# Gated products woven into the second attention of a two-layer gated cross-attention kernel

## The chip, the cores and the metric

The kernel runs on one core of a Trainium2 chip. The metric is the device time of one execution in microseconds (us). Three runs of the kernel before took 686.56, 687.71 and 687.75 us; the median, 687.71, is what a changed kernel is held against.

## What is computed

Two layers work on x (2 batches of 1024 tokens, 256 features) with a context of 77 tokens. All numbers are fp32. Cut to what matters:

```python
x = x + tanh(g_xattn[0]) * differential_attention(ctx, layernorm(x))       # layer 0: 32 half heads of 8
x = x + tanh(g_ffn[0]) * zone_ffn(layernorm(x))                            # router takes 3 of 8 zones, gelu, 1024 wide
x = x + tanh(g_xattn[1]) * (softmax(q @ k.T / 4) @ v @ Wo + bo)            # layer 1: 16 heads of 16, q from layernorm(x)
x = x + tanh(g_ffn[1]) * ((silu(gate) * up) @ wd.T)                        # gate = x @ wg.T, up = x @ wu.T, 768 wide,
                                                                           # int weights times 1/127, x normed
```

## The kernel before

**Tiles and stages.** The 2048 tokens are four tiles of 512 (J = 4); a tile is four blocks of 128 tokens. The stages are ATT0, FFN0, ATT1 and FFN1. A product in fp32 precision is made of three passes over parts rounded to fp32r: high times high, low times high, high times low (`product`, L1163, its matmuls at L1167). So each operand has a high part, written by ScalarE (ACT) as a copy, and a low part, raw minus high, written by VectorE (DVE).

**What sets the order.** `plan()` (L118) writes one list of steps by hand. Each engine walks through the whole list and issues its share of every step in that order, with semaphores between the engines. A step moved in the list is moved on every queue. `attention_tile` (L74) lays out one tile of an attention: eight `attend` units of two heads, and after each second unit a `values` and an `outputs` step of the pair before; `side` holds steps that come after a given unit and `fillers` steps that are spread over the gaps. `weave` (L59) does the same for the zone and gated stages.

**The second attention, steps by engine.** `attend` is two matmuls of 512 columns into one of two pairs of score banks, SC (L1302); ACT takes their exp into a probability buffer PB of 77 rows (L815). `values` is 32 matmuls of 128 columns on 32-column tiles into PV bank 0 (L1187); DVE transposes it (`outputs`, L1059) and takes reciprocals (`mix`, L1065); GpSimd (POOL) adds the output bias to x ahead of the first mix of a tile (L686) and multiplies (L692). `max` is two matmuls of 154 columns (L1274) and a DVE reduction (L1051); `negmax` turns the maxima (L1285), ACT copies them and SP moves them into the query tile. `query` makes twelve matmuls, and `q_move` moves its parts on the DMA queues of SP (L543), for tile 2 of this attention half of them on POOL (L659). `turn_mix` is eight transposes of the attention result, `project` 24 matmuls of 256 columns with Wo and an addition on DVE (L1127). For the norm ahead of FFN1, `stats` and `norm` are on DVE and POOL (L969, L982, L630), `scale` is four activations (L760), `turn` eight transposes, two copies and two low parts.

**The gated stage.** Its weights come as int32 by `ffn_load` (L582), into one of two buffers, and are split in six halves by `ffn_split` (ACT L884, DVE L911). A `gated` step s works on one of six chunks of a tile: twelve matmuls for gate and up into a pair of SC banks, silu on ACT (L892), a product on DVE (L1142), its high part on ACT (L728) and its low part on DVE (L911), and two steps later the down product, six matmuls into PV (`gated_out`, L1204). `evac` copies the sums with the gate's factor (L874), `out` turns them back with eight transposes (L1352), adds to x (L1114), and SP stores the tile (L587).

**Banks.** PSUM has eight banks: SC four, PV two, AUX two. Turns, queries, maxima and the like go through a ring of auxiliary banks: AUX 0, AUX 1 and PV 1 in the attentions, the two AUX in the zone and gated stages.

**What the change touches.** In `plan()` the whole second attention and gated stage, L213 to L257; the ring of banks, L275 to L289; in the engines' programs the branches `ffn_load`, `out`, `mix`, `attend`, `ffn_split`, `gated`, `turn`, `query`, `turn_mix`, `project` and the helpers `bank`, `fill`, `attend_values`, `gated_out`, `gated_hi`. The order before, from plan(), of the first steps behind the third attend of tile 2 was: max, norm, attend, max, values, max, outputs, max, ffn_split, scale, attend; no gated step came before the last values of tile 3.

## Time and profile before

| | us |
|---|---|
| median of three runs | 687.71 |
| the profiled execution, its own time | 686.08 |
| its span, first to last instruction | 684.2 |
| second attention: first attend to first gated matmul | 484.4 to 568.6 |
| gated stage, to its last matmul | 568.6 to 678.4 |
| evac, out and store of the last tile | 678.4 to 684.2 |

The profiled execution is one more run; its span is its time less what lies around the instructions. In the rows, PE is the matrix engine (PEld its weight loads, which overlap it), ACT ScalarE, DVE VectorE, POOL GpSimd, SP the engine that only issues DMAs. PEclk is the granted clock of PE as a share of 2.4 GHz. "idle before <-" is how long an engine stood idle ahead of an instruction and who released it; L numbers are lines of the kernel before.

### The profile page before, as it was taken

How to read it: one execution, taken by the hardware profiler on the slowest of the kernel's cores; microseconds unless marked ns; L12 is line 12 of the kernel's file. 1: busy time of each engine (PE TensorE's matmuls, PEld its weight loads, DVE VectorE, ACT ScalarE, POOL GpSimd, SP SyncE). 2: the span in 40 equal slices, each digit the busy share in tenths (PEclk: the TensorE clock that was granted, in tenths of full speed). 3: DMA queues.
4: the chain of work that ended last, by engine and by line, in shares of the span. 5: the costliest groups of instructions: out<-in, count | busy, mean ns of one | idle time of the engine just before them, and what ended most of it. 6: DMA issues, size and time to landing. Idle time of an engine off the chain costs nothing.

```text
span 684.2 us, 10256 instructions
## 1 busy us (share of the span) xinstructions
PE 621.6 (91%) x3676; PEld 479.4 (70%) x3676; DVE 369.2 (54%) x817; ACT 370.0 (54%) x631; POOL 142.6 (21%) x212
## 2 busy tenths in 40 slices
PE   2699888898799999999999999999789889999996
PEld 2575555554478888888887787778577767888885
DVE  6677667779573524335456435443477655343332
ACT  4316757566775746556657445446746564243232
POOL 9633265354640000000000000001245222000000
PEclk9769999999999999999999999999978699999999
DMA  7320120112130030300312430000343000000000
GB/s 229 97 77 21 32 60 11 46 49 97 31 122 4 0 124 0 123 2 0 124 32 62 94 123 2 2 0 2 94 140 94 3 2 1 1 31 1 32 31 32
DMA packets 21970, 34.68 MB, mean 51 GB/s; under 512 B 4640, under 2 KB 13216, under 8 KB 21920
## 3 DMA queue, kind: packets, MB, share of 16 engines
q1 hardware_dynamic: 19648, 30.51, 14.3%
q0 software_dynamic: 1984, 3.44, 2.2%
q8 instruction: 30, 0.49, 0.3%
q14 instruction: 20, 0.16, 0.1%
q10 hardware_dynamic: 288, 0.07, 0.0%
HBM read 18.93 MB, written 2.10 MB: 31 GB/s over the span
## 4 chain that ended last, share of the span: by engine, by line
PE 76%; DVE 8%; POOL 6%; ACT 6%; issue 3%; DMA 0%; DVEq 0%; ACTq 0%; POOLq 0%
PE SC L1167 28%; PE PV L1167 26%; PE PV L1187 5%; PE AUX L1167 4%; PE SC L1302 4%; PE AUX L1274 3%; ACT XN L760 2%; DVE NM L1051 2%; DVE O L1059 2%; PE AUX L1230 2%; PE PV L1274 1%; POOL RSTD L630 1%; DVE ST L969 1%; ACT PB L815 1%; POOL QG L659 1%
## 5 line engine op out<-in xcount | busy, mean ns | idle before, releaser
L911 DVE TENSOR_TENSOR HL<-HF,HH 128x512 fp32r<-128x512 f32 x120 | 83.7, 698 | 154.1 <-ACT HH L857 153.8
L815 ACT ACTIVATE PB<-SC 77x1024 f32<-77x1024 f32 x96 | 94.3, 1014 | 46.5 <-PE SC L1302 46.2
L857 ACT ACTIVATE HH<-PV 128x512 fp32r<-128x512 f32 x96 | 57.3, 597 | 66.8 <-PE SC L1167 66.8
L852 ACT ACTIVATE HF<-PV 128x512 f32<-128x512 f32 x96 | 57.3, 597 | 54.8 <-PE PV L1167 53.0
L630 POOL TENSOR_TENSOR RSTD<-RSTD,NHALF 128x4 f32<-128x4 f32 x16 | 17.4, 1089 | 321.8 <-DVE RSTD L982 321.7
L1167 PE MATMUL PV<-XH,WAH 128*128 128x512 f32 x192 | 77.7, 404 | 1.0 <-DVE O L1059 1.0
L1167 PE MATMUL SC<-HH,WBH 128*128 128x512 f32 x192 | 76.3, 397 | 0.0
L1167 PE MATMUL SC<-HH,WBL 128*128 128x512 f32 x192 | 75.7, 394 | 0.0
L1167 PE MATMUL PV<-XL,WAH 128*128 128x512 f32 x192 | 75.4, 393 | 0.0
L1167 PE MATMUL PV<-XH,WAL 128*128 128x512 f32 x192 | 75.3, 392 | 0.0
L1167 PE MATMUL SC<-HL,WBH 128*128 128x512 f32 x192 | 74.9, 390 | 0.0
L1302 PE MATMUL SC<-QG,KA 128*128 128x512 f32 x192 | 67.9, 444 | 4.2 <-ACT PB L815 3.1
L1051 DVE TENSOR_REDUCE NM<-AUX 128x4 f32<-128x308 f32 x139 | 62.0, 465 | 11.3 <-PE AUX L1274 11.3
L1274 PE MATMUL AUX<-KA,QG 96*128 96x154 f32 (+1 forms) x192 | 51.0, 335 | 10.2 <-DVE NM L1051 6.0
L1274 PEld LDWEIGHTS AUX<-KA,QG 96*128 96x128 f32 x192 | 37.1, 211 | 27.8 <-DVE NM L1051 12.2
L1187 PE MATMUL PV<-PB,V 128*32 128x256 f32 (+1 forms) x1024 | 54.5, 345 | 1.7 <-DVE O L1059 1.6
L892 ACT ACTIVATE SG<-SC 128x512 f32<-128x512 f32 x24 | 14.3, 596 | 68.7 <-PE SC L1167 68.7
L1142 DVE SCALAR_TENSOR_TENSOR HF<-SC,SG 128x512 f32<-128x512 f32 x24 | 16.6, 692 | 59.8 <-ACT SG L892 59.8
L1302 PEld LDWEIGHTS SC<-QG,KA 128*128 128x128 f32 x192 | 33.0, 204 | 13.9 <-issue 7.7
L1187 PEld LDWEIGHTS PV<-PB,V 128*32 128x32 f32 (+1 forms) x1024 | 28.0, 114 | 21.0 <-issue 9.6
L1167 PEld LDWEIGHTS PV<-XH,WAH 128*128 128x128 f32 x192 | 36.1, 188 | 8.6 <-issue 1.8
L1167 PEld LDWEIGHTS SC<-HH,WBL 128*128 128x128 f32 x192 | 36.0, 188 | 8.7
(241 smaller groups left out, 1214.8 us busy)
## 6 DMA issues: line engine op xcount, KB each, us to landing
QG<-QH SPq DMA_DIRECT2D x96, 64.0 KB, 2.0
WSA<-in_wa SPq DMA_DIRECT2D x6, 1024.0 KB, 5.1
...
```

Of the source, the lines that this page charges most:

```text
L630: pool.tensor_tensor(RSTD[:, 1, :], RSTD[:, 0, :], NHALF[:, :], ALU.pow).then_inc(pool_step, 1)
L815: act.activation(probs(n)[0:S, :, :], SC[0:S, n % 2, :, :], ACT.Exp, scale=SCALE[a]).then_inc(exp_done, 1)
L852: act.activation(HF[s % 2][:, :], PV[:, s % 2, :], ACT.Gelu_apprx_tanh)
L857: act.activation(HH[s % 2][:, :], PV[:, s % 2, :], ACT.Gelu_apprx_tanh).then_inc(act_done, 1)
L892: act.activation(SG[s % 2][:, :], SC[:, s % 2, 0, :], ACT.Silu, scale=DEQ).then_inc(silu_done, 1)
L911: return dve.tensor_tensor(dst, raw, hi.bitcast(F32), ALU.subtract)
L1051: dve.tensor_reduce(NM[:, n % 2, t, 4 * u:4 * u + 4], bank(key)[:, 0:4 * S].rearrange("p (h n) -> p h n", h=4), AX_X, ALU.max, negate=True ...
L1142: dve.scalar_tensor_tensor(HF[s % 2][:, :], SC[:, s % 2, 1, :], DEQ, SG[s % 2][:, :], ALU.mult, ALU.mult).then_inc(hf_ready, 1)
L1167: ins = pe.matmul(ps, lhs, rhs, start=start and i == 0, stop=stop and i == len(passes) - 1)
L1187: ins = pe.matmul(PV[32 * r:32 * r + 32, 0, at_h:at_h + P * (heads.stop - heads.start)], v, p[:, heads, :, r, :], start=True, stop=True)
L1274: ins = pe.matmul(ps[:, i * n_cols:(i + 1) * n_cols], QG[n % 2][0:ROWS, g, P * t:P * (t + 1)], KA[a][0:ROWS, j // 2, NS[a] * g:NS[a] * (g ...
L1302: ins = pe.matmul(SC[:, n % 2, i, :], KALL[a][:, at_h:at_h + P], QG[m % 2][:, h // NS[a], :], start=True, stop=True)
```

## The change

The steps `turn`, `query`, `turn_mix`, `project` and `out` are cut into their halves. The `gated` step becomes three: `gated_g` (six matmuls), `gated_u` (six matmuls) and `gated_mul`, and the down product a step `gated_out`. Behind attend 2 of tile 2 the list blends the gated steps 0 to 5 with the rest of tile 2 of the attention, then steps 6 to 11 with tile 3 and the attention's end, by the loads in LOAD; steps 12 to 23 follow alone. While they are woven, the attention has one pair of score banks (SC 0) and the gated steps the other (SC 1); the down sums go to PV 1 and AUX 1; the auxiliary ring is AUX 0 alone from the first down product to step 12, then AUX 0 and PV 0. Silu is computed from a tanh: SG = tanh(gate/2), then (SG + 1) * gate on DVE, then times up on DVE. The first two weight loads go into the last zone of FFN0, four of the six splits into tile 0, two into tile 1. The norm ahead of FFN1 comes two to three units after its project, and project, turn_mix come earlier. The values read all 128 rows, so POOL clears the rows from 64 on of the buffers at the end of FFN0. POOL's bias add waits for the norm of its tile and no longer for the reciprocals. The result is stored in eight halves instead of four tiles.

```diff
@@ -51,6 +51,9 @@
 ATT0, FFN0, ATT1, FFN1 = range(4)
 SMALL = 13
 LAG = 2
+MIXED = 2 * HC
+PARTS = {"turn": (3, KC), "query": (3, KC), "turn_mix": (2, KC), "project": (2, 2), "out": (3, 2)}
+LOAD = {"attend": 2, "values": 3, "max": 1, "negmax": 2, "turn": 2, "turn_mix": 2, "project": 3, "out": 2}
...
+def blend(main, items):
+
+    items, out, given = parted(items), [], 0
+    total = sum(LOAD.get(step[0], 0) for step in items)
+    for n, atom in enumerate(main):
+        out += atom
+        while items and (given * len(main) < total * (n + 1) or not LOAD.get(items[0][0], 0)):
+            given += LOAD.get(items[0][0], 0)
+            out.append(items.pop(0))
+    return out + items
+
+
+def gated_atoms(first, last):
+
+    atoms = []
+    for s in range(first, last):
+        atoms += [[("gated_g", s)], [("gated_u", s), ("gated_mul", s)]]
+        if s >= LAG:
+            atoms.append([("gated_out", s - LAG)])
+            if (s - LAG) % HC == HC - 1:
+                atoms[-1] += [("evac", FFN1, (s - LAG) // HC)]
+    return atoms
...
+    side.setdefault(per * (Z - 2) + FC + FC - 1 + LAG + 3, []).extend([("ffn_load", 0), ("ffn_load", 1)])
...
+    def at(side, u, *more):
+        side.setdefault(u, []).extend(more)
+    def behind(side, j, base):
+        at(side, base, ("turn_mix", j, 0))
+        at(side, base + 1, ("turn_mix", j, 1))
+        at(side, base + 2, ("project", j))
+        for i, step in enumerate(norm(FFN1, j)):
+            at(side, base + 3 + i // 3, step)
+        at(side, base + 5, ("scale", FFN1, j))
+    side = {}
+    at(side, 0, *norm(ATT1, 3))
+    at(side, 1, ("ffn_split", 0, 0))
+    at(side, 2, ("scale", ATT1, 3))
+    at(side, 3, ("q_move", 1, 2, 0), ("ffn_split", 0, 1), ("ffn_load", 2))
+    at(side, 4, ("turn", ATT1, 3))
+    at(side, 5, ("ffn_split", 1, 0))
+    at(side, 7, ("q_move", 1, 2, 1), ("ffn_split", 1, 1))
+    steps += attention_tile(1, 0, side, [], left)
+    side = {}
+    at(side, 1, ("ffn_split", 2, 0))
+    behind(side, 0, 1)
+    at(side, 3, ("ffn_split", 2, 1))
+    at(side, 4, ("negmax", 1, 2, 0))
+    at(side, 5, ("query", 1, 3))
+    at(side, 6, ("q_move", 1, 3, 0))
+    at(side, 7, ("negmax", 1, 2, 1))
+    steps += attention_tile(1, 1, side, [(maxima(1, 2, 0), 0, 3), (maxima(1, 2, 1), 4, 7)], left)
+    side = {}
+    at(side, 0, ("q_move", 1, 3, 1), ("turn", FFN1, 0, 0))
+    at(side, 1, ("turn", FFN1, 0, 1))
+    behind(side, 1, 1)
+    at(side, 5, ("negmax", 1, 3, 0))
+    at(side, 7, ("turn", FFN1, 1))
+    items = attention_tile(1, 2, side, [(maxima(1, 3, 0), 1, 5), (maxima(1, 3, 1), 5, 8)], left)
+    alone = items.index(("attend", 1, 2, 2)) + 1
+    steps += items[:alone] + blend(gated_atoms(0, HC), items[alone:])
+    side = {}
+    at(side, 0, ("negmax", 1, 3, 1))
+    behind(side, 2, 1)
+    at(side, 5, ("out", FFN1, 0, 0))
+    at(side, 6, ("out", FFN1, 0, 1))
+    at(side, 7, ("turn", FFN1, 2))
+    items = attention_tile(1, 3, side, [], left) + attention_end(left)
+    steps += blend(gated_atoms(HC, MIXED), items)
+    side = {}
+    at(side, 1, ("turn_mix", 3, 0))
+    at(side, 3, ("turn_mix", 3, 1))
+    at(side, 5, ("project", 3))
+    at(side, 6, *norm(FFN1, 3))
+    at(side, 7, ("out", FFN1, 1, 0))
+    at(side, 8, ("scale", FFN1, 3), ("out", FFN1, 1, 1))
+    at(side, 12, ("turn", FFN1, 3, 0))
+    at(side, 13, ("turn", FFN1, 3, 1))
+    at(side, 25, ("out", FFN1, 2, 0))
+    at(side, 26, ("out", FFN1, 2, 1))
+    for n, atom in enumerate(gated_atoms(MIXED, HC * J)):
+        steps += atom + side.get(n, [])
+    end = HC * J
+    steps += [("gated_g", end), ("gated_u", end), ("gated_mul", end), ("gated_out", end - 2), ("gated_out", end - 1),
+              ("evac", FFN1, 3), ("out", FFN1, 3)]
+    return parted(steps)
...
+    home, uses, turn_now, ring = {}, [0, 0, 0, 0], 0, (0, 1, 2)
+    lent, last_in = [], {}
     for step in PLAN:
         order[step] = seen.get(step[0], 0)
         seen[step[0]] = order[step] + 1
-        if step[0] in ("zone", "gated"):
-            banks = 2
+        if step[0] == "zone":
+            ring = (0, 1)
         elif step == ("attend", 1, 0, 0):
-            banks = 3
+            ring = (0, 1, 2)
+        elif step == ("gated_out", 0):
+            ring = (0,)
+        elif step == ("gated_g", MIXED):
+            ring = (0, 3)
...
-            return AUX[:, n, :] if n < 2 else PV[:, 1, :]
+            return AUX[:, n, :] if n < 2 else PV[:, 3 - n, :]
...
+        MIXED_UNITS = unit(1, 2, 0)
+        SUMS = (PV[:, 1, :], AUX[:, 1, :])
+
+        def scores(n):
+
+            return SC[:, n % 2 if n < MIXED_UNITS else 0, :, :]
+
+        def gate(s):
+
+            return SC[:, 1 if s < MIXED else s % 2, :, :]
...
                 elif kind == "ffn_load":
                     i = step[1]
-                    sp.wait_ge(y_done, ZSTEPS)
                     sp.wait_ge(zsplit_done, FC * Z)
                     if i == 2:
                         sp.wait_ge(fsplit_done, 2)
                     dst = WI[i % 2][:, :].rearrange("p (c n) -> p c n", c=HC if i == 2 else KC)
                     sp.dma_start(dst, chunks((wg, wu, wd)[i])).then_inc(ffn_in[i], 16)
                 elif kind == "out" and step[1] == FFN1:
-                    j = step[2]
-                    for i in range(2):
-                        used(sp, step + (i,))
-                    sp.dma_start(out[j], X[:, TT * j:TT * (j + 1), :]).then_inc(stored, 16)
-            sp.wait_ge(stored, 16 * J)
+                    _, _, j, i = step
+                    used(sp, step)
+                    sp.dma_start(out[j][:, 2 * i:2 * i + 2, :],
+                                 X[:, TT * j + 2 * i:TT * j + 2 * i + 2, :]).then_inc(stored, 16)
+            sp.wait_ge(stored, 16 * 2 * J)
...
+                elif kind == "zone_end":
+                    pool.wait_ge(rstd_ready, sum(NORMS.index(s) < NORMS.index(("norm", ATT1, 3)) for s in NORMS))
+                    pool.wait_ge(hl_ready, ZSTEPS)
+                    pool.memset(PB2[1][1][64:P, :, :], 0.0).then_inc(pb_set, 1)
+                    pool.memset(PB2[1][0][64:P, :, :], 0.0).then_inc(pb_set, 1)
+                    for s in range(2):
+                        pool.wait_ge(y_done, ZSTEPS - 1 + s)
+                        pool.memset(PB[0][64:P, s, :], 0.0).then_inc(pb_set, 1)
+                        pool.memset(PB[1][64:P, s, :], 0.0).then_inc(pb_set, 1)
+                    pool.wait_ge(pb_set, 10)
...
+                            pool.wait_ge(xn_ready, order["norm", ATT1, j] + 1)
...
+                        pool.wait_ge(rz_ready, n + 1)
...
-                        act.wait_ge(y_done, ZSTEPS)
-                    act.activation(probs(n)[0:S, :, :], SC[0:S, n % 2, :, :], ACT.Exp, scale=SCALE[a]).then_inc(exp_done, 1)
+                        act.wait_ge(pb_set, (9, 10, 10, 10)[n - A0_UNITS])
+                    act.activation(probs(n)[0:S, :, :], scores(n)[0:S, :, :], ACT.Exp, scale=SCALE[a]).then_inc(exp_done, 1)
...
                 elif kind == "ffn_split":
                     _, i, h = step
                     act.wait_ge(ffn_in[i], 16)
+                    act.wait_ge(y_done, ZSTEPS)
                     dst, src, rows = ffn_half(i, h)
                     act.activation(dst[0][:, rows, :], src, copy).then_inc(fsplit_hi, 1)
-                elif kind == "gated":
+                elif kind == "gated_u":
                     s = step[1]
-                    act.wait_ge(g_ready, s + 1)
-                    if s >= 2:
-                        act.wait_ge(hf_ready, s - 1)
-                    else:
-                        act.wait_ge(sc_ready, ALL_UNITS)
-                    act.activation(SG[s % 2][:, :], SC[:, s % 2, 0, :], ACT.Silu, scale=DEQ).then_inc(silu_done, 1)
                     if s:
-                        gated_hi(s - 1)
-                elif kind == "gated_end":
-                    gated_hi(GSTEPS - 1)
+                        act.wait_ge(hf_ready, s)
+                        if s >= 3:
+                            act.wait_ge(gy_done, s - 2)
+                        else:
+                            act.wait_ge(fsplit_done, 6)
+                        act.activation(GH[(s - 1) % 2][:, :], GF[(s - 1) % 2][:, :], copy).then_inc(ghh_ready, 1)
+                    if s < GSTEPS:
+                        act.wait_ge(g_ready, s + 1)
+                        if s >= 2:
+                            act.wait_ge(hf_ready, s - 1)
+                        else:
+                            filled(act, ("query", 1, J - 1, KC - 1))
+                        act.activation(SG[s % 2][:, :], gate(s)[:, 0, :], ACT.Tanh, scale=0.5 * DEQ).then_inc(tanh_done, 1)
...
+                elif kind == "gated_g":
+                    s = step[1] - 1
+                    if s >= 0:
+                        dve.wait_ge(ga_done, s + 1)
+                        dve.wait_ge(u_ready, s + 1)
                         if s >= 2:
                             dve.wait_ge(ghl_ready, s - 1)
                         else:
-                            dve.wait_ge(pv_done, ALL_UNITS // 2)
-                        dve.scalar_tensor_tensor(HF[s % 2][:, :], SC[:, s % 2, 1, :], DEQ, SG[s % 2][:, :],
+                            dve.wait_ge(fsplit_done, 6)
+                        dve.scalar_tensor_tensor(GF[s % 2][:, :], SG[s % 2][:, :], 0.5 * DEQ * DEQ, gate(s)[:, 1, :],
                                                  ALU.mult, ALU.mult).then_inc(hf_ready, 1)
+                elif kind == "gated_mul":
+                    s = step[1]
                     if s:
                         dve.wait_ge(ghh_ready, s)
                         if s >= 3:
                             dve.wait_ge(gy_done, s - 2)
-                        lo_part(HL[(s - 1) % 2][:, :], HF[(s - 1) % 2][:, :], HH[(s - 1) % 2][:, :]).then_inc(ghl_ready, 1)
+                        lo_part(GL[(s - 1) % 2][:, :], GF[(s - 1) % 2][:, :], GH[(s - 1) % 2][:, :]).then_inc(ghl_ready, 1)
+                    if s < GSTEPS:
+                        dve.wait_ge(tanh_done, s + 1)
+                        dve.scalar_tensor_tensor(SG[s % 2][:, :], SG[s % 2][:, :], 1.0, gate(s)[:, 0, :],
+                                                 ALU.add, ALU.mult).then_inc(ga_done, 1)
...
-                rows = slice(0, P) if a == 0 else slice(0, S)
                 for i in range(2):
-                    p = probs(2 * q + i)[rows, :, :].rearrange("s i (t q r) -> s i t q r", t=TT, r=32)
+                    p = probs(2 * q + i)[:, :, :].rearrange("s i (t q r) -> s i t q r", t=TT, r=32)
                     for n in range(1 if a == 0 else 2):
                         heads = slice(0, 2) if a == 0 else slice(n, n + 1)
                         at_v = (j // 2 * (D // DV) + (2 * k + i if a == 0 else 4 * k + 2 * i + n)) * (DV + 1)
-                        v = VALL[a][rows, at_v:at_v + 32]
+                        v = VALL[a][:, at_v:at_v + 32]
...
-                        pe.wait_ge(pv_out, ALL_UNITS // 2)
-                        used(pe, LENT[1][-1])
+                        for n in (1, 2):
+                            used(pe, last_in[n])
...
-                    ins = product(PV[:, c, :], [(WNH[:, f, cols], WNL[:, f, cols], HH[s % 2][:, :], HL[s % 2][:, :])],
+                    ins = product(SUMS[c], [(WNH[:, f, cols], WNL[:, f, cols], GH[s % 2][:, :], GL[s % 2][:, :])],
...
+                    if n > MIXED_UNITS:
+                        pe.wait_ge(exp_done, n)
...
+                elif kind in ("gated_g", "gated_u") and step[1] < GSTEPS:
+                    cols = slice(P * f, P * (f + 1))
+                    if kind == "gated_g":
+                        if f == 0:
+                            pe.wait_ge(fsplit_done, 4)
+                            for c in range(KC):
+                                used(pe, ("turn", FFN1, j, c))
+                        if s in (0, MIXED):
+                            pe.wait_ge(exp_done, ALL_UNITS if s else MIXED_UNITS)
+                        else:
+                            pe.wait_ge(ga_done, s if s < MIXED else s - 1)
+                        product(gate(s)[:, 0, :], [(WGH[:, c, cols], WGL[:, c, cols], XH[:, j, c, :], XL[:, j, c, :])
+                                                   for c in range(KC)]).then_inc(g_ready, 1)
+                        if s not in (0, MIXED):
+                            pe.wait_ge(hf_ready, s if s < MIXED else s - 1)
+                        product(gate(s)[:, 1, :], [(WUH[:, c, cols], WUL[:, c, cols], XH[:, j, c, :], XL[:, j, c, :])
+                                                   for c in range(KC)]).then_inc(u_ready, 1)
+                elif kind == "gated_out":
+                    gated_out(step[1])
```

## Rows read from the trace of the kernel before

**Rows 1.** The page, busy us of PE, share of the span, instructions
```profile
PE 621.6 (91%) x3676; PEld 479.4 (70%) x3676; DVE 369.2 (54%) x817; ACT 370.0 (54%) x631; POOL 142.6 (21%) x212
```

**Rows 2.** Windows by stage: busy us (instructions) of each engine, clock, DMA share, GB/s
```profile
484.40:496.50 12.10, 9.30 (x124) 5.74 (x121) 5.81 (x17) 10.46 (x14) 5.00 (x9) 1.00 0.47 145
505.20:516.50 11.30, 11.30 (x66) 9.15 (x67) 5.34 (x11) 2.29 (x3) 2.38 (x1) 0.55 0.25 72
526.30:530.00 3.70, 2.52 (x42) 1.95 (x40) 3.67 (x8) 2.84 (x4) 1.05 (x1) 1.00 0.36 89
530.00:543.00 13.00, 10.54 (x66) 8.83 (x67) 7.84 (x21) 6.07 (x10) 2.08 (x3) 0.50 0.01 2
568.60:678.40 109.80, 108.21 (x508) 88.62 (x504) 44.82 (x84) 38.09 (x69) 3.49 (x5) 1.00 0.04 15
```

**Rows 3.** Timeline: start us, us, engine, line, instruction [idle before <-releaser]
```profile
485.18 2.92 ACT L815 ACTIVATE PB<-SC 77x1024 f32<-77x1024 f32 x3 [2.04 <-PE SC L1302]
...
495.74 2.38 POOL L686 TENSOR_TENSOR X<-X,BOG 128x1024 f32<-128x1024 f32 x1 [3.49 <-DVE RZ L1065]
...
502.09 2.00 DVE L911 TENSOR_TENSOR WGL<-WI,WGH 128x768 fp32r<-128x768 int32 x1
502.19 1.07 POOL L692 TENSOR_TENSOR MIX<-O,RZ 128x512 f32<-128x512 f32 x1
...
505.18 0.43 PE L1274 MATMUL PV<-KA,QG 96*128 96x154 f32 x2 [1.93 <-issue]
...
530.39 0.71 PE L1274 MATMUL AUX<-KA,QG 96*128 96x154 f32 x2 [1.58 <-DVE NM L1051]
```

**Rows 4.** Chain of waits: start us, us, pieces of packed work
```profile
539.90 1.07 PE AUX L1274 x4
...
545.04 1.01 PE PV L1187 x32
...
576.41 2.75 PE SC L1167 x12
579.16 1.37 PE PV L1167 x6
...
584.69 0.87 PE AUX L1360 x8
...
593.86 2.73 PE AUX L1167 x24
```

**Rows 5.** The gated weights' tile: ns min/median/max, first and last start
```profile
L884 ACT ACTIVATE WGH<-WI x2: 833/835/837, 499.1 to 502.7; 128x768 fp32r<-128x768 int32 x2
L911 DVE TENSOR_TENSOR WGL<-WI,WGH x2: 910/1455/2000, 502.1 to 505.0; 128x768 fp32r<-128x768 int32 x2
```

**Rows 6.** Groups by line: count | busy us, mean ns | idle before, releaser
```profile
L815 ACT ACTIVATE PB<-SC 77x1024 f32<-77x1024 f32 x96 | 94.3, 1014 | 46.5 <-PE SC L1302 46.2
...
L1051 DVE TENSOR_REDUCE NM<-AUX 128x4 f32<-128x308 f32 x139 | 62.0, 465 | 11.3 <-PE AUX L1274 11.3
...
L892 ACT ACTIVATE SG<-SC 128x512 f32<-128x512 f32 x24 | 14.3, 596 | 68.7 <-PE SC L1167 68.7
L1142 DVE SCALAR_TENSOR_TENSOR HF<-SC,SG 128x512 f32<-128x512 f32 x24 | 16.6, 692 | 59.8 <-ACT SG L892 59.8
...
L1059 DVE STREAM_TRANSPOSE O<-PV 128x512 f32<-128x512 f32 x48 | 34.0, 709 | 13.6 <-PE PV L1187 13.6
...
L674 POOL MEMSET PB<- 64x1024 f32 x4 | 3.6, 950 | 0.0
```

**Rows 7.** Timeline around the gated stage and at its end
```profile
565.29 1.28 ACT L892 ACT_TABLE_LOAD   x1
...
575.31 1.09 PE L1230 MATMUL AUX<-ident,XN 128*128 128x128 f32 x8 [0.95 <-ACT XN L760]
...
675.37 0.50 PE L1167 MATMUL PV<-HH,WNH 128*128 128x512 f32 x1 [0.62 <-DVE HL L911]
...
681.22 0.33 SPq L587 DMA_DIRECT2D out_x<-X  x1
```

276 lines of the change are left out of this document (100 added, 176 removed).

## The prediction

> **What bounds the kernel now.** I read the page's busy table first: the matrix engine PE is busy for 621.6 of 684.2 us, so the time falls only where PE waits or runs slowly [rows 1]. The windows by stage say where. In the gated stage (568.6 to 678.4 us) PE is busy for 108.2 of 109.8 us at clock 1.00, beside 44.8 us of VectorE (DVE) and 38.1 of ScalarE (ACT). The second attention is different: PE sits idle in places, and in three stretches the clock is at or near its lower level (1.2 of 2.4 GHz); the two long ones read 0.55 and 0.50 [rows 2]. An idle PE stands just ahead of both: 1.93 us ahead of the first, with no holder that the profile shows, and 1.58 us for a maximum on DVE ahead of the second [rows 3]. So the tail of the attention has PE time to give, and the gated stage has ACT and DVE time to give. The chain of waits then gives what a piece of PE work takes when it is packed [rows 4].
>
> **Mark.** I count from the end of attend unit 2 of tile 2, 526.3 us before, where a window of rows 2 begins. Three parts follow: A ahead of it, B the woven part (gated steps 0 to 11), C from gated step 12 to the end. Before, 157.9 us follow the mark.
>
> **A, up to the mark.** Four splits of gated weights come into tile 0 of the attention, three ahead of its last exp. ACT is busy for 10.46 of 12.1 us there, with 1.64 us idle: 3 x 0.835 less about 0.5 of slack is +2.0 us [rows 2, 5]. DVE has 6.3 us free there and takes four splits of about 0.95. Two FFN1 turns and one turn_mix come ahead of the mark, 3 x 0.44: +1.3 [rows 4]. The stall of 1.93 us at 503.25 goes. It ends when the second half of tile 2's queries has landed. POOL issued its share of those moves up to 502.2 us, the start of its next mix; they stood behind its bias add (2.38 us, begun at 495.74 once the reciprocals were there) and a mix [rows 3]. The bias add no longer waits for reciprocals (3.49 us of idle POOL in its row), and the two weight loads that ran beside the moves are now issued in the first FFN: -1.9. The late landing is next behind the ACT work of tile 0. The slow stretch that follows (11.3 us at 0.55, so some 5.1 us lost) is not settled by any row. If it stays the term is 0, if it goes it is -5.1. The stall ahead of it goes, but tile 0 gets sparser for PE; its window held 1.00 at 9.3 busy of 12.1 [rows 2]. I take the middle, -2.6. A: 526.3 + 2.0 + 1.3 - 1.9 - 2.6 = 525.1 us.
>
> **B, the woven part.** PE work at full clock, by the chain's rows, each with the 0.01 or 0.02 to its successor [rows 4]: gate and up of 12 steps at 2.76 = 33.1; ten down products at 1.39 = 13.9; 13 attends of two 512-column matmuls at 2.76/12 each = 6.0; eight values at 1.01 = 8.1; 13 maxima at 0.27 (1.07 for two of them, four matmuls, at half clock) = 3.5; nine sets of four transposes (turn, turn_mix, negmax) at 0.44 = 4.0; one out 0.9; two projects at 2.73 = 5.5. Sum 75.0 us. DVE gets in B, by [rows 6]: 12 additions-and-products and 12 products at 0.69, 11 low parts at 0.7 (the same length and type), eight transposes at 0.71, 13 reductions at 0.47, and some 15 us of low parts, projects, norms and outs, together about 51 us. ACT: 13 exps at 1.02, 12 tanh and 11 copies, and 12 us more of scales, high parts and copies, about 39. PE is the longest, but the attention and the gated steps now hold only one pair of score banks each, and from the first down product on one auxiliary bank where three were. So waits come back. (a) Attends 4 and 5 of tile 3 stand side by side in the plan, and the second needs the first's exp: 1.3 us. (b) One auxiliary bank: two places where a fill follows a maximum at once (reduction and hand-over, 0.7 each), three where a turn's second half waits for copy and low part of the first (1.6 us against 1.38 of cover): 2.1 us. (c) Changes between 32-column and full products at eight values, and work that comes late in the in-order queues of ACT and DVE, above all a scale of four activations ahead of a tanh: no row has these for B, I allow 4.6. Waits of 8 us; bounds 3 (only (a) and what the plan's neighbours force) and 20 (below). A gated step's loop, tanh 0.60, product 0.69 and hand-overs, is 1.6 us against 2.8 us of up and down products beside it, so it waits for nothing while the queues are short.
>
> **Cheap edits.** Tanh in place of silu: the row of silu at the same shape gives 0.60 [rows 6], so nothing (no row has a tanh of this size; were it 0.3 longer, C's ACT would still be at 2 us of each 4.15); the extra DVE product (0.69 a step) hides under C's PE work, where DVE goes from 1.4 to 2.1 us of each 4.15; without that cover it costs 0.69 x 12 = 8.3. The table load of 1.28 us ahead of the first silu stood in idle ACT time and goes for nothing [rows 7]. Clearing halves of the probability buffers on POOL: 0.95 for a whole one [rows 6], half of one each for the last two, which follow the last matmuls of the first FFN; ACT then stood idle for 2.04 us ahead of the first exp at 485.18 [rows 3], so 0; without that idle time they would cost 1 us. Values over 128 rows instead of 77: the same 32 matmuls of 128 columns, 0, with the clock as the unknown. The waits added to the splits and to the first exps are over when reached. SP issues the two big loads behind negmax of tile 0 and ahead of that of tile 1, with 17 us to spare; 0.
>
> The first low part of a gated step has two SBUF inputs, and it now runs beside POOL's adds. The row that bears on this is the low part of WG, 2.00 us beside a mix on POOL and 0.91 without it [rows 3, 5]. POOL works for some 12 of B's 83 us (two bias adds, four mixes, two norms), so about 1.6 of the 11 low parts meet it, 1.7 us of DVE time, inside (c). The Trainium skill, page SBUF — State Buffer, section Who interferes with whom, says that a VectorE instruction with two SBUF inputs contends with a GpSimd instruction that reads SBUF. It speaks against this weave, and the row agrees; by it, were all 11 to meet POOL, B would get 12 us more on DVE instead of 1.7.
>
> **C and the end.** 12 x 2.76 + 14 x 1.39 + turn_mix 0.87 + project 2.73 + turn 0.88 + two outs 1.7 = 58.7 us [rows 4]. Before, the gated stage lost 0.95 us ahead of a turn and 0.62 us behind its last gate matmul, where the second last low part stood behind the last product on DVE [rows 7]; in the new order it stands ahead, so 58.7 holds no wait. From the last matmul to the end: 5.8 us before; with half tiles the first half leaves early and 256 KB instead of 512 are left, the gain between 0 and 1.5 (half of the 3.0 us from the last issue at 681.22 to the end [rows 7]); I take 0.4, near 0, since no row has a store of 256 KB: 5.4.
>
> **Sum.** 525.1 + 75.0 + 8 + 58.7 + 5.4 = 672.2 against 684.2: 12.0 us less. The profiled execution took 686.08, its span and 1.9 us around it; the sum gives 674.1 for one like it. The median of the runs shown is 687.71, 1.6 above, so on that scale I forecast 675.7 us. About 0.2%, 1.4 us, is what a measurement can tell from no change.
>
> **Rivals.** R1, more: the slow stretch of A goes whole (another -2.5) and the waits are only 4 us: 669.2. For it: both long slow stretches follow a stall. Against: one auxiliary bank. R2, less: DVE's queue runs late wherever a norm, a turn and a gated product meet, waits of 16 us: 683.7. For it: from 526.3 to 530.0 DVE was busy for 3.67 of 3.70 us and PE for 2.52 [rows 2]. Against: over all of B DVE is at 51 of 83. R3, slower: the gated steps' loop closes on the one pair of banks. Were every step to wait 2.0 us (tanh 0.60 and product 0.69 behind one exp or low part, nothing of it covered), 24 us of waits replace my 8: 691.7. It decides from 8 + 12 = 20 us, 1.67 a step. Against: up and down products cover 2.8. R4, the clock: micro-waits of B bring PE to the lower level, as in 530 to 543, where 13 us at 0.50 held some 5 us too much [rows 2]; two or three such stretches give 686 to 691. The Trainium skill, page TensorE: Matmul & The Clock Gate, section A second HAM failure mode: psum-queue depth-cycling, tells of a kernel in which short idles at each change of PSUM bank made the clock go back and forth; rows 2 and 3 show falls behind idles, but not behind such short ones. Against: gate and up are six matmuls in a row each, and their stage never fell.
>
> **Chances.** Forecast (671 to 680) 0.46, R1 0.22, R2 0.16, R3 0.07, R4 0.07, and 0.02 that the weave only shifts the waits and nothing changes. Within 0.2% fall 0.01 of R2, 0.02 of R4 and the last 0.02; of R4 0.02 lie below that and 0.03 above. So faster 0.46 + 0.22 + 0.15 + 0.02 = 0.85, the same 0.05, slower 0.07 + 0.03 = 0.10. Range 667 to 685: forecast, R1 and 0.14 of R2, together 0.82; it takes in the clock of A (2.5 either way), waits of 3 to 17 us and the bounds of the end.
>
> **What would show it.** The mark near 525 with no stall of 2 us in tile 1; PE in B at 1.00 with some 8 us idle; the first gate matmul right behind the mark, gated step 12 near 608; C without a wait until the last down product; no table load before tanh; the end 5.4 us behind the last matmul. Wrong if B shows a clock below 0.9, if PE waits for ga or for exps by over 1.5 us a step, or if the mark comes after 530.

## The result, and the profile after

The changed kernel takes 682.44 us (median of four runs, 680.97 to 683.2), the kernel before 687.13 (four runs, 686.45 to 687.75): ratio 0.9937, 95% interval [0.991, 0.9963]. It is faster by 4.7 us. I had forecast 675.7, 12 us less. The side is right and the time lies in the range, but the gain is 0.4 of the forecast one. A second measurement (e13 below) gave 0.9942 [0.9921, 0.9963].

The page of after, busy us of each engine (beside [rows 1]):
```profile
PE 614.7 (91%) x3676; PEld 470.5 (69%) x3676; DVE 385.6 (57%) x841; ACT 369.5 (54%) x630; POOL 147.5 (22%) x218
```
Windows of after by stage (columns as in [rows 2]): first attend to tile 2, to the first gated matmul, to gated step 12, to the last matmul; then tile 0, and the head of tile 2 in two pieces:
```profile
483.63:520.70 37.07, 30.20 (x351) 22.21 (x350) 29.12 (x62) 25.30 (x34) 18.74 (x24) 1.00 0.26 70
520.70:530.82 10.12, 6.85 (x60) 5.23 (x57) 4.35 (x9) 6.84 (x11) 5.95 (x12) 0.83 0.53 144
530.82:614.47 83.65, 78.33 (x605) 62.00 (x605) 47.12 (x94) 35.72 (x56) 10.21 (x9) 1.00 0.02 8
614.47:673.86 59.39, 59.25 (x285) 48.41 (x283) 33.51 (x58) 22.10 (x38) 2.63 (x3) 1.00 0.05 19
...
483.63:497.79 14.16, 9.34 (x124) 5.76 (x122) 10.20 (x20) 13.10 (x18) 7.27 (x10) 1.00 0.31 83
...
520.70:525.00 4.30, 1.74 (x11) 1.04 (x9) 0.50 (x1) 4.23 (x7) 4.30 (x10) 1.00 0.69 200
525.00:530.82 5.82, 5.11 (x51) 4.19 (x49) 3.85 (x8) 2.61 (x4) 1.65 (x3) 0.71 0.41 104
```
The same windows of before, to the first attend of tile 2, the first gated matmul, gated step 12 and the last matmul:
```profile
484.39:523.15 38.76, 33.81 (x352) 25.53 (x349) 24.32 (x49) 24.63 (x32) 19.73 (x29) 0.87 0.43 127
523.15:568.59 45.44, 38.84 (x443) 31.57 (x441) 28.68 (x63) 28.09 (x37) 12.64 (x13) 0.81 0.07 17
568.59:623.06 54.47, 53.52 (x264) 44.40 (x261) 25.52 (x54) 21.11 (x39) 3.49 (x5) 1.00 0.03 11
623.06:678.38 55.32, 54.70 (x245) 44.23 (x243) 19.30 (x31) 16.95 (x30) 0.00 (x0) 1.00 0.05 20
```
The woven part and what is behind it run at clock 1.00. Tiles 0 and 1 do too, where before they read 0.87. The trouble stands at the head of tile 2: of its first 4.30 us PE works 1.74, ACT 4.23, and then the clock falls (0.71). The timeline of after there:
```profile
519.86 2.07 ACT L845 ACTIVATE XN<-X,RSTD 128x256 f32<-128x256 f32 x4
...
521.82 1.01 ACT L898 ACTIVATE PB<-SC 77x1024 f32<-77x1024 f32 x1
...
522.86 0.59 ACT L885 ACTIVATE NMT<-PV 8x512 fp32r<-8x512 f32 x1
...
523.47 1.02 ACT L898 ACTIVATE PB<-SC 77x1024 f32<-77x1024 f32 x1
...
524.64 0.71 PE L1389 MATMUL SC<-QG,KA 128*128 128x512 f32 x2 [2.00 <-ACT PB L898]
...
525.46 1.84 PE L1273 MATMUL PV<-PB,V 128*32 128x128 f32 x32
...
529.39 0.72 PE L1389 MATMUL SC<-QG,KA 128*128 128x512 f32 x2
...
530.82 0.47 PE L1254 MATMUL SC<-XH,WGH 128*128 128x512 f32 x1 [0.71 <-DVE XL L999]
```
Scaling, exp, copy, exp: ACT has a queue without a gap, and attend unit 1 of tile 2 (524.64) waits for its end. My mark, the end of attend unit 2, is at 530.11.

### The profile page after: what moved, and what is told of

Same layout as the page of the kernel before. It is cut to its first block, busy times and chain, and to the rows that moved or that the text cites. A ratio compares the mean times of both kernels' runs of the same rounds, so it can differ in the third digit from the quotient of the medians.

```text
span 679.2 us, 10341 instructions
## 1 busy us (share of the span) xinstructions
PE 614.7 (91%) x3676; PEld 470.5 (69%) x3676; DVE 385.6 (57%) x841; ACT 369.5 (54%) x630; POOL 147.5 (22%) x218
## 4 chain that ended last, share of the span: by engine, by line
PE 74%; DVE 11%; ACT 6%; POOL 5%; issue 4%; DMA 0%; ACTq 0%; DVEq 0%; POOLq 0%
PE SC L1254 29%; PE PV L1254 24%; PE AUX L1254 6%; PE PV L1273 4%; PE AUX L1359 3%; PE SC L1389 3%; DVE NM L1135 2%; DVE O L1143 2%; ACT XN L845 2%; ACT PB L898 1%; PE AUX L1316 1%; DVE ST L1057 1%; PE PV L1359 1%; POOL QG L739 1%; DVE XL L999 1%
## 5 line engine op out<-in xcount | busy, mean ns | idle before, releaser
L999 DVE TENSOR_TENSOR HL<-HF,HH 128x512 fp32r<-128x512 f32 x96 | 67.4, 702 | 153.8 <-ACT HH L940 153.7
L1389 PE MATMUL SC<-QG,KA 128*128 128x512 f32 x192 | 65.4, 428 | 7.9 <-ACT PB L898 6.1
L1135 DVE TENSOR_REDUCE NM<-AUX 128x4 f32<-128x308 f32 x144 | 64.0, 465 | 14.3 <-PE AUX L1359 14.2
L1273 PEld LDWEIGHTS PV<-PB,V 128*32 128x32 f32 x1024 | 27.5, 112 | 22.2 <-issue 9.7
L1254 PEld LDWEIGHTS PV<-XH,WAL 128*128 128x128 f32 x192 | 36.1, 188 | 8.5
L1254 PEld LDWEIGHTS SC<-HL,WBH 128*128 128x128 f32 x192 | 36.1, 188 | 8.4
```

The costliest lines, as they stand in the source:

```text
L999: return dve.tensor_tensor(dst, raw, hi.bitcast(F32), ALU.subtract)
L1135: dve.tensor_reduce(NM[:, n % 2, t, 4 * u:4 * u + 4], bank(key)[:, 0:4 * S].rearrange("p (h n) -> p h n", h=4), AX_X, ALU.max, negate=True ...
L1254: ins = pe.matmul(ps, lhs, rhs, start=start and i == 0, stop=stop and i == len(passes) - 1)
L1273: ins = pe.matmul(PV[32 * r:32 * r + 32, 0, at_h:at_h + P * (heads.stop - heads.start)], v, p[:, heads, :, r, :], start=True, stop=True)
L1389: ins = pe.matmul(scores(n)[:, i, :], KALL[a][:, at_h:at_h + P], QG[m % 2][:, h // NS[a], :], start=True, stop=True)
```

## The experiments

Each was timed beside the kernel before on its chip; e1 to e4 share a chip, so do e5 to e8, e9 to e11, and e12 to e15. "Gain" is one less the ratio; after has 0.6%. In the table are each profiled execution's stretches (us, clock): from the first attend to tile 2, from there to gated step 12, and the whole span.

| kernel | ratio [95%] | to tile 2 | to step 12 | span |
|---|---|---|---|---|
| before | 1 | 38.76, 0.87 | 99.91 | 684.2 |
| after | 0.9937 [0.991, 0.9963] | 37.07, 1.00 | 93.77 | 679.2 |
| after again, e13 | 0.9942 [0.9921, 0.9963] | 38.11, 0.96 | 94.52 | 681.6 |
| e1_two_pairs | 0.9937 [0.9916, 0.9958] | 37.15, 1.00 | 93.18 | 678.8 |
| e2_77_rows | 0.9984 [0.9965, 1.0003] | 39.33, 0.87 | 95.70 | 684.6 |
| e3_silu | 1.0002 [0.9979, 1.0026] | 37.03, 1.00 | 96.65 | 683.7 |
| e4_bias_late | 1.0026 [1.0007, 1.0046] | 38.45, 0.91 | 99.85 | 688.3 |
| e5_before_128 | 0.9947 [0.9924, 0.997] | 35.15, 1.00 | 99.93 | 681.2 |
| e6_no_weave | 0.999 [0.9969, 1.0011] | 37.15, 1.00 | 98.83 | 681.4 |
| e7_whole_store | 0.9952 [0.9928, 0.9976] | 37.05, 1.00 | 96.06 | 682.8 |
| e8_both | 0.9949 [0.9926, 0.9971] | 39.42, 0.87 | 93.99 | 684.4 |
| e9_before_128_bias | 0.9967 [0.9946, 0.9987] | 35.16, 1.00 | 99.69 | 680.1 |
| e10_splits_later | 0.9961 [0.9943, 0.998] | 38.14, 0.96 | 94.64 | 681.8 |
| e11_later_start | 0.991 [0.9886, 0.9933] | 37.96, 0.96 | 92.70 | 679.2 |
| e12_query_early | 0.9894 [0.9874, 0.9913] | 38.15, 1.00 | 89.18 | 676.9 |
| e14_maxima_late | 0.9947 [0.9926, 0.9968] | 37.14, 1.00 | 93.12 | 680.3 |
| e15, e11 again | 0.9919 [0.9895, 0.9943] | 37.14, 1.00 | 91.88 | 678.7 |

One kernel's clock differs from one execution to the next (after and e13 are the same code: span 679.2 and 681.6). So single profiles show where time goes, and ratios say how much.

**e1: the head of tile 2 as a matter of banks.** Attends of tile 2 keep two pairs of score banks up to the third:
```diff
-        MIXED_UNITS = unit(1, 2, 0)
+        MIXED_UNITS = unit(1, 2, 0) + 2
```


> The first two attends of tile 2 use both score pairs, as they do in tiles 0 and 1; the single pair starts at attend 2, where the gated steps begin. Theory S (the part of the forecast that failed is the head of tile 2: attend 1 stands idle for 2.00 us because its one score pair waits for an exp behind the scaling on ACT, and the clock falls behind that idle, 0.66 in 525 to 530): the idle goes, the clock stays at 1.00, 3 to 5 us less than the changed kernel, about 678. Rival Q (ACT's queue is late anyway, so the idle only moves to the turn or to attend 2): within 1 us of 682.4, with the same slow stretch.


The ratio is after's. Attend unit 1 now waits 0.34 us instead of 2.00, but the next maximum waits 0.90 us for a landing of tile 3's queries, and the first gated matmul comes 9.45 us behind the start of tile 2 instead of 10.12:
```profile
523.20 0.71 PE L1389 MATMUL SC<-QG,KA 128*128 128x512 f32 x2 [0.34 <-ACT PB L898]
...
524.82 0.42 PE L1359 MATMUL AUX<-KA,QG 96*128 96x154 f32 x2 [0.90 <-DMA QG<-QH]
```
So the bank was a holder, as theory S says, but not at its price; ACT's queue and the landing are still there.

**e2 and e5: the rows that the values read.** e2 is after with the values over 77 rows again, e5 is before with 128 rows, the clearing on POOL and the wait of the first exps for it, and nothing else.
```diff
+                rows = slice(0, P) if a == 0 else slice(0, S)
...
-                        v = VALL[a][:, at_v:at_v + 32]
+                        v = VALL[a][rows, at_v:at_v + 32]
```
```diff
...
-                rows = slice(0, P) if a == 0 else slice(0, S)
+                rows = slice(0, P)
```


> The values of the second attention read 77 rows again, all else as changed. If the rows read have no part in the clock: within 1 us of the changed kernel and mean clock 0.98. Rival R (reading 128 rows is what keeps the clock up from 500 to 525): stretches near 0.5 come back in tiles 0 and 1 and it takes 4 to 6 us more, about 687, with mean clock 0.97 or less.

> The kernel before with one part of the change alone: its values read 128 rows (with POOL's clearing at the end of the first FFN). If the slow stretches of before came from the idle ahead of them only: unchanged, within 1 us of 687, with clock near 0.55 and 0.50 in 505 to 516 and 530 to 543. Rival R (rows read hold the clock): the slow stretches shrink or go, 5 to 10 us less, 677 to 682, which would be as much as the whole change gave.


e5 has nearly the whole gain of the change, 0.5%, and e2 loses 0.5% of it. The windows up to tile 2 and to the first gated matmul, e5:
```profile
484.96:520.11 35.15, 29.96 (x352) 22.04 (x350) 23.63 (x49) 24.61 (x32) 19.65 (x29) 1.00 0.47 139
520.11:565.55 45.44, 38.21 (x443) 30.75 (x441) 28.69 (x63) 28.11 (x37) 12.79 (x13) 0.85 0.07 18
```
Tiles 0 and 1 take 3.6 us less than before and show no fall of the clock; the second window is as long as before's. All of the 3.6 is PE's busy time (29.96 for 33.81); it is idle for 5.2 us in that window, before for 5.0. Of 17 profiled executions the two with 77 rows read 0.87 there; of the 15 with 128 rows ten read 1.00, the others 0.87 to 0.96. The mean clock of whole runs says the same: the twelve of e2 read 0.959 to 0.975, the nine of e1 on the same chip 0.977 to 0.982. So the rows make the fall rarer, they don't exclude it.

**e3: silu on ACT again.** The ACT gives silu at once, without the addition-and-product on DVE.
```diff
-                        act.activation(SG[s % 2][:, :], gate(s)[:, 0, :], ACT.Tanh, scale=0.5 * DEQ).then_inc(tanh_done, 1)
+                        act.activation(SG[s % 2][:, :], gate(s)[:, 0, :], ACT.Silu, scale=DEQ).then_inc(ga_done, 1)
...
-                        dve.scalar_tensor_tensor(SG[s % 2][:, :], SG[s % 2][:, :], 1.0, gate(s)[:, 0, :],
-                                                 ALU.add, ALU.mult).then_inc(ga_done, 1)
```


> Silu is taken from ACT's table again and the extra product on DVE goes. By the table load of 1.28 us in the rows of before, and about two loads for each of the woven steps (exp, silu, exp), 12 to 24 loads come into the woven part: 15 to 31 us of ACT. Theory T (ACT then is late for exps and silus): 8 to 20 us more than the changed kernel, 690 to 702. Rival U (ACT has 45 us free in the woven part and DVE is what is late): the loads hide, the missing 0.69 us per step of DVE pays, 1 to 4 us less.


Exp and silu now take turns, and each turn loads a table. The groups of e3:
```profile
L984 ACT ACT_TABLE_LOAD x11 | 14.1, 1283 | 0.2
L898 ACT ACT_TABLE_LOAD x10 | 12.8, 1283 | 0.2
```
21 loads, 27 us more on ACT, and B takes 86.34 us instead of 83.65. The whole gain is gone (1.0002), but of 27 us only some 4.5 are seen (686.24 us for 681.86 of e1 on the same chip), with the product of 0.69 us a step on DVE saved: ACT had room. Tanh, which needs no load here, is worth that.

**e4 and e9: the bias add.** In e4 it waits for the reciprocals again; e9 is e5 with it made early, in the code of before.
```diff
-                            pool.wait_ge(xn_ready, order["norm", ATT1, j] + 1)
+                            pool.wait_ge(rz_ready, n + 1)
```


> POOL's bias add waits for the reciprocals again, as before the change. If my term of -1.9 us was right, its mix and its share of the moves of tile 2's queries come 2 to 4 us later and a stall comes back in tile 1: 1.5 to 3 us more. Rival: with the weight loads out of the way and tile 0 longer by 2 us the moves are in time anyway: within 0.7 us.

> The kernel before with two parts of the change and no more: the values read 128 rows (as in e5_before_128), and POOL adds the bias before the reciprocals are there instead of behind them. Theory H (the two parts that make the second attention run without a wait and without a fall of the clock carry the gain; the weave gives little of its own): the wait of about 2 us in tile 1 goes on top of the gain of e5, and tile 1 to the start of the gated steps gets some 2 to 3 us shorter: ratio to the kernel before 0.990 to 0.992, so as fast as the whole change or faster. Rival W (the weave is what gives the gain of the whole change, and the bias add matters only because the woven steps wait for it): ratio as e5, 0.994 to 0.996.


e4 is the slowest of all: 1.0026, some 6 us above after, not the 1.9 of my step; in its profiled execution, the slowest of its twelve, 4 us lie in B (87.91 for 83.65). But e9 gains nothing over e5. What the early add does shows in two places. The first is the stall of 1.93 us before [rows 3]. It ends at the first maximum that reads the second half of tile 2's queries, and POOL moves the last part of that half. The move and its time to landing, before and in e9:
```profile
501.68 0.50 POOL L659 DMA_DIRECT2D QG<-QH  x1
QG<-QH POOLq DMA_DIRECT2D x1, 64.0 KB, 3.4
...
499.00 0.50 POOL L659 DMA_DIRECT2D QG<-QH  x1
QG<-QH POOLq DMA_DIRECT2D x1, 64.0 KB, 3.9
502.94 0.30 PEld L1286 LDWEIGHTS PV<-KA,QG 96*128 96x128 f32 x2 [0.45 <-DMA QG<-QH]
502.97 0.42 PE L1286 MATMUL PV<-KA,QG 96*128 96x154 f32 x2
```
Before, it lands at 505.1 and the maximum starts at 505.18; in e9 it lands at 502.9 and the same maximum starts at 502.97, without a stall of PE. Counted from the first attend of tile 1 the landing comes 8.6 us in before and 6.7 in e9. So the stall was that of the landing: in both kernels the maximum starts 0.1 us behind it, and the early add takes the stall away. In e5 the add is late, but the last move (502.32) lands after 1.9 us, 504.2, before PE gets there. e9 has another wait in its place, two maxima later, where before has none:
```profile
502.31 3.08 POOL L696 TENSOR_TENSOR X<-X,BOG 128x1024 f32<-128x1024 f32 x1
...
504.11 2.10 DVE L923 TENSOR_TENSOR WGL<-WI,WGH 128x768 fp32r<-128x768 int32 x1
506.14 0.47 DVE L1063 TENSOR_REDUCE NM<-PV 128x4 f32<-128x308 f32 x1
...
506.66 0.45 PE L1286 MATMUL PV<-KA,QG 96*128 96x154 f32 x2 [1.88 <-DVE NM L1063]
```
The low part of WG runs beside the early add, the reduction stands behind it on DVE, and PE waits for the reduction. PE is idle in tile 1 for 2.2 us before and for 2.3 in e9: what the early add saves it takes back.

The second place is tile 0. In after the early add runs beside a low part, and the transpose of the values stands behind that low part:
```profile
491.58 2.40 POOL L776 TENSOR_TENSOR X<-X,BOG 128x1024 f32<-128x1024 f32 x1
...
492.02 2.79 DVE L999 TENSOR_TENSOR WGL<-WI,WGH 128x768 fp32r<-128x768 int32 x1 [3.02 <-ACT WGH L968]
...
496.77 1.08 PE L1273 MATMUL PV<-PB,V 128*32 128x128 f32 x32 [1.21 <-DVE O L1143]
```
In e4, with the add later, the same low part takes 0.96 us, that wait of PE is gone, and tile 0 takes 12.91 us instead of 14.16:
```profile
493.68 0.96 DVE L999 TENSOR_TENSOR WGL<-WI,WGH 128x768 fp32r<-128x768 int32 x1 [3.01 <-ACT WGH L968]
...
497.16 1.08 PE L1273 MATMUL PV<-PB,V 128*32 128x128 f32 x32
```
In tile 1 of e4 the add and the mix behind it run beside another low part (1.50 us), and PE waits 1.66 us for the reduction behind that.

**e6: all but the weave.** The gated steps stand behind the attention again, the rest is as after.
```diff
-MIXED = 2 * HC
+MIXED = 0
...
-    steps += items[:alone] + blend(gated_atoms(0, HC), items[alone:])
+    steps += items
...
-    steps += blend(gated_atoms(HC, MIXED), items)
+    steps += items
```


> All of the change but the weave: the 24 gated steps stand behind the attention, three auxiliary banks and two score pairs through it, tanh, early loads and splits, half stores. By my sum the woven part's work is 75 us plus 8.8 of waits; apart, the rest of the attention has 28 us of work in which PE waits for 8 to 14 us. So the weave itself is worth 2 to 6 us: this kernel 684 to 689. Rival W (the weave pays for nothing, the gain of 4.7 us is the clock of tiles 0 and 1 alone): the same as the changed kernel or below it, 678 to 683.


0.999: without the weave the other parts bring 0.1%, the weave with its head brings 0.5%. The rows of e5, one of those parts, bring 0.5% alone on the same chip, so the rest of them take that back: up to tile 2 e6 needs 37.15 us and e5 35.15, the 2 us of tile 0. The profiled execution, the lowest of its runs, shows how thin this is: 46.29 us at clock 0.96 from tile 2 to the first gated matmul and 107.41 behind it are 153.70, after has 153.16.

**e7 and e8.** e7 stores each tile whole; e8 is e1 with the statistics and norms of FFN1 put behind the gate matmuls where they stood within three steps ahead of them.
```diff
-                    sp.dma_start(out[j][:, 2 * i:2 * i + 2, :],
-                                 X[:, TT * j + 2 * i:TT * j + 2 * i + 2, :]).then_inc(stored, 16)
+                    if i:
+                        sp.dma_start(out[j], X[:, TT * j:TT * (j + 1), :]).then_inc(stored, 16)
```
```diff
-    return parted(steps)
+    return later_norms(parted(steps))
```


> The result is stored in whole tiles of 512 KB again. By the ends of the two traces (5.8 us from the last matmul before, 5.3 after) 0.3 to 0.6 us more than the changed kernel. Rival: the two half stores at the end share what they gain with one more issue: no difference.

> Two score pairs until attend 2 of tile 2, and in the woven part the statistics and the norm stand behind the product on DVE that frees the up bank, not ahead of it. In the trace of the changed kernel PE stands idle at 547.5, 556.5 and 601 for 1 to 3 us each while DVE works on statistics, norm and the late product. If that order is the cause, 2 to 4 us less than with the two pairs alone, about 675 if those give 678. Rival: the product is late for other reasons (in-order DVE full), then no more than 0.7 us less than the two pairs alone.


e7: from the last matmul to the end 5.9 us instead of 5.3, so half tiles are worth 0.6 (I took 0.4). The ratio can't tell it from after, nor e8's, so the 2 to 4 us that I expected of e8's order did not come.

**e10: two splits out of tile 0.**
```diff
-    at(side, 5, ("ffn_split", 1, 0))
-    at(side, 7, ("q_move", 1, 2, 1), ("ffn_split", 1, 1))
+    at(side, 7, ("q_move", 1, 2, 1))
...
-    at(side, 1, ("ffn_split", 2, 0))
+    at(side, 0, ("ffn_split", 1, 0))
+    at(side, 1, ("ffn_split", 1, 1))
```


> The kernel after with the two splits of the second gated weight moved from tile 0 of the second attention to tile 1, and the splits of the third behind them. My prediction's step: three splits on ScalarE in tile 0 cost 2.0 us. If that step holds and tile 1 has the slack that its windows show (ScalarE and VectorE at some 60 to 80 percent), tile 0 takes 12.4 to 12.8 us instead of 14.16, and the time falls by 1.3 to 1.8 us: ratio to the kernel before about 0.991 to 0.992. Rival: the head of tile 2 is bound by ScalarE, the splits arrive there late, and what tile 0 gives is lost again: ratio 0.993 to 0.995.


Tile 0 takes 14.51 us with ACT at 11.94, no less than with ACT at 13.10, and the ratio is no better. Three splits and 2.06 us came together in after, but ACT's sum is not what tile 0 waits for: PE waits 1.21 us here too, behind the same low part, 2.78 us beside the early add.

**e11, e12, e14: the head of tile 2.** e11 puts the scaling behind the first exp of tile 2, its turns and the first gated step two attends later. e12 adds that tile 3's queries are formed two attends earlier, e14 instead that its maxima are asked for later (the three diffs in this order, the last two against e11). All three also keep the two pairs of banks of e1. e13 is after and e15 is e11, unchanged, on the chip of e12 and e14.
```diff
-    at(side, 0, ("q_move", 1, 3, 1), ("turn", FFN1, 0, 0))
-    at(side, 1, ("turn", FFN1, 0, 1))
+    at(side, 0, ("q_move", 1, 3, 1), ("scale", FFN1, 0))
+    at(side, 2, ("turn", FFN1, 0, 0))
+    at(side, 3, ("turn", FFN1, 0, 1))
...
-    alone = items.index(("attend", 1, 2, 2)) + 1
+    alone = items.index(("attend", 1, 2, 4)) + 1
```
```diff
-    at(side, 5, ("query", 1, 3))
-    at(side, 6, ("q_move", 1, 3, 0))
+    at(side, 3, ("query", 1, 3))
+    at(side, 4, ("q_move", 1, 3, 0))
```
```diff
-    at(side, 5, ("negmax", 1, 3, 0))
+    at(side, 6, ("negmax", 1, 3, 0))
...
-    items = attention_tile(1, 2, side, [(maxima(1, 3, 0), 1, 5), (maxima(1, 3, 1), 5, 8)], left)
+    items = attention_tile(1, 2, side, [(maxima(1, 3, 0), 3, 6), (maxima(1, 3, 1), 6, 8)], left)
```


> The kernel after, with the weave begun later: the four scaling activations for the first gated tile stand behind the first exp of tile 2 and not at the end of tile 1, its turns two attends later, and the first gated step behind attend 4 of tile 2 instead of attend 2; two pairs of banks up to the second attend of tile 2, as in e1. Theory A (the head of tile 2 is bound by the chain of ScalarE: exp, four scalings of 2.07 us together, exp, copy, exp, and this stall of 2.0 us ahead of an attend brings the clock down): the attend that waited 2.0 us for an exp waits under 0.7, the clock in the 5 us behind it stays above 0.9, and the time falls by 1.5 to 3 us against the kernel after: ratio to before 0.989 to 0.992. Rival (the work is only moved; ScalarE has as much to do before the first gated step, and PE has less to stand beside it): no change against after, 0.993 to 0.996, or a loss of up to 2 us.

> e11 with one thing more: the queries of tile 3 are formed two attends earlier in tile 1, and their first half is moved two attends earlier. Theory M (behind the chain of ScalarE stands the landing of tile 3's first half of queries: the maxima of tile 3 waited 2.60 us for it in e11): that wait is under 0.7 us, PE has no idle stretch of 2 us between 519 and 530, and the clock of that stretch reads above 0.9; time 1 to 3 us below that of e11. Rival C (the clock falls there whatever single wait is taken away, because PE has little work between the attends while ScalarE has its 5 us): the wait of 2.60 goes, but the stretch from 520 to 530 still holds a fall, and the time is within 1 us of e11.

> e11 with one thing more: the maxima of tile 3's first half are asked for two attends later in tile 2 (those of the second half one later, and the move of the maxima one later). Theory M: the wait of 2.60 us at the first of them goes, as in e12, and PE idles for ScalarE alone; time 0.5 to 2 us below that of e11. Rival C: PE has still less to do at the head of tile 2, the idle time only moves to the attends, and the time is that of e11 or up to 2 us more; in addition the attends of tile 3 may wait for the late maxima.

> The kernel after, unchanged, on the same chip as e12, e14 and e15: what the four ratios are to be compared with. Its first ratio was 0.9937 [0.991, 0.9963]; I expect 0.993 to 0.996.

> The kernel of e11 once more, beside the kernel after on the same chip. If the later start of the weave is worth what e11 showed, its ratio to the kernel before is 0.990 to 0.993 and some 0.2 to 0.4 percent (1.5 to 3 us) below that of e13; if the 680.92 us of e11 was the luck of one call, the two ratios agree within 0.1 percent.


In e11 the wait for the exp is gone, and another stands in its place; the clock of 525 to 530 is 0.50. The timeline of e11:
```profile
525.61 0.71 PE L1361 MATMUL AUX<-KA,QG 96*128 96x154 f32 x2 [2.60 <-DMA QG<-QH]
```
In e12 the landing costs 0.78 us (theory M said under 0.7), and the stretch holds clock 1.00:
```profile
525.01 0.45 PE L1361 MATMUL AUX<-KA,QG 96*128 96x154 f32 x2 [0.78 <-DMA QG<-QH]
```
Windows of e12 as for after:
```profile
484.90:523.05 38.15, 29.77 (x351) 22.29 (x350) 29.43 (x62) 25.44 (x33) 19.37 (x26) 1.00 0.29 80
523.05:536.26 13.21, 11.60 (x131) 9.70 (x129) 8.24 (x17) 8.57 (x13) 6.91 (x10) 1.00 0.30 76
536.26:612.23 75.97, 71.54 (x533) 56.23 (x532) 42.67 (x86) 33.62 (x53) 8.22 (x8) 1.00 0.02 8
612.23:671.60 59.37, 59.24 (x285) 48.41 (x283) 33.49 (x58) 22.09 (x38) 2.64 (x3) 1.00 0.05 19
```
From tile 2 to step 12 it takes 89.18 us against 93.77 and 94.52 of after. Time: 678.87 us against 682.69 of after on the same chip; e11's edit alone (e15) 680.17. The two repeats came as expected (0.9942 and 0.9919). So the later start is worth some 2.5 us by itself, seen on two chips but with intervals that overlap after's, and the early queries 1.3 more. The intervals of e12 (0.9874 to 0.9913) and of after (0.9921 to 0.9963) don't touch; e12 is 1.1% faster than before and beats both kernels. e14 holds the clock as well, and its wait for the landing is gone, but it takes 682.22 us, 2 more than e15, where theory M forecast 0.5 to 2 less: from the first gated matmul to step 12 it takes 79.91 us against 76.04 in e11, 1.6 of it PE's work that moved there and 2.2 idle time, and the ratio is after's. Theory M is borne out by e12 and missed in e14, where the time came back later; rival C had named that time, but for a fall of the clock that isn't there. e12's first window holds one more us than after's: what the early queries cost.

## Why the prediction was wrong in size

Summed as I did, with the measured terms of the profiled execution: mark 530.11 (forecast 525.1), from the mark to step 12 84.36 (75.0 + 8 = 83.0), C 59.39 (58.7), end 5.3 (5.4): 679.2 instead of 672.2. Of the 7.0 us missed 5.0 are in A.

- **A is the step that failed, by what I left out of it: the head of tile 2.** The terms that I named sum well, in part by luck. The first attend came 0.8 earlier. Tile 0 cost +2.06 (I said +2.0), but not by ACT's splits alone: 1.25 of it go in e4, with the late add, where PE no longer waits behind the low part of 2.79 us. Tile 1 took 22.91 us instead of 26.66 (497.79 to 520.70; before, 496.49 to 523.15), 3.75 less for my 4.5 (stall and middle of the clock). But from the start of tile 2 to the mark it took 9.41 us, before 3.15: 6.3 more, for which I had set two turns and half a turn_mix, 1.3. I had moved the scaling of four activations ahead of the exps of tile 2 without laying ACT's queue out there, though I named just this danger for B. e11 and e12 show that two holders stood behind each other, ACT's queue and the landing of tile 3's queries: with the first moved the time falls by some 2.5 us, with both by 3.8. The clock goes with them only in part: the head reads 0.80 and 0.89 in e11 and e15, 1.00 in e12 and e14, but 1.00 in e8 and e10 too, whose ratios are no better than after's.
- **The stall of 1.93 us** was read rightly: it is the landing of tile 2's queries, and e9 shows that the early add moves that landing ahead of the need. In after the last part lands at 504.4 (501.17 and 3.2 us), 6.6 us behind the first attend of tile 1 instead of 8.6, and the maximum that reads it stands behind `turn_mix` and `project`, at 510.53, so the new list alone would have hidden it too. But the -1.9 is not there: PE is idle in tile 1 for 2.05 us in after and for 2.15 before. The rest of the 3.75, 3.65 us, is its busy time (20.86 for 24.51), the clock. I gave the early add no price where it meets low parts on DVE: 1.25 us in tile 0. Even so, undone in the woven order it costs some 6 us (e4), by its one profile the larger part of them in B, and the reason there is not shown.
- **The values over 128 rows: "0, with the clock as the unknown"** was the worst-sized edit. By e5 it is worth 0.5% alone, by e2 as much when undone. The -2.6 for the clock in A stands for 3.65 us; I tied that fall to the stall. In e5 the idle time is as before and the fall is gone.
- **B.** PE works 78.33 us there, not 75.0, and idles 5.3 in it (0.7 more ahead of it), not 8; together 84.36 for my 83.0, 1.4 too little. (a) is there as forecast: 1.20 us at 595.76 for the exp of the adjacent attend. (b) reads 1.23 at 567.16 (a turn behind a maximum) and 1.62 at 571.54 (a gate matmul behind the low part of the turn), 2.9 us for 2.1. The clock is 1.00. Tanh costs 0.59, silu had 0.60 [rows 6], and no table load is left in the stretch.
```profile
567.16 0.63 PE L1316 MATMUL AUX<-ident,XN 128*128 128x128 f32 x4 [1.23 <-DVE NM L1135]
571.54 0.47 PE L1254 MATMUL SC<-XH,WGH 128*128 128x512 f32 x1 [1.62 <-DVE XL L999]
595.76 0.70 PE L1389 MATMUL SC<-QG,KA 128*128 128x512 f32 x2 [1.20 <-ACT PB L898]
```
- **C and the end** as forecast, 59.39 and 5.3. The 0.7 of C lies in PE's work: it was busy for 59.25.
- **Rivals.** R2 had nearly the right total (683.7 for my scale's 682.4) by another way: its 16 us of waits in B were not there. R3 decides at 20 us and R4 needs falls in B; neither came. R1's half is true: the slow stretch of tile 1 did go whole in this execution. The rule of the Trainium skill, page SBUF — State Buffer, section Who interferes with whom, that a VectorE instruction with two SBUF inputs contends with a GpSimd instruction that reads SBUF, bore on this case, at another place than I put it. In B only one of the 11 low parts of a product met POOL (1.17 us at 582.44, the others 0.65 to 0.69; I had said 1.6 of them), but the weights' low part takes 0.91 us alone and 2.79 in after beside the bias add. The trace agrees in the other direction too: at 581.01 a low part with one input in PSUM stands whole beside the bias add and takes 0.69.
- **My list** said: wrong if the mark comes after 530. It came at 530.11. Step 12 was late with it (614.47 for 608), and the idle time in B was 5 us for 8; the rest of the list held.

What stays open: why rows of zeros that the values read keep the clock up, and why B takes 4 us more in e4, with the late bias add. The parts don't add: e2, e3, e4 and e6 each undo one and lose 0.5 to 0.9 of a gain of 0.6%. That they share the clock is a reading of the table and was not shown by itself.
